# Laying down the engine orders of a four-stage attention kernel from new durations, and moving 32 PSUM copies to ScalarE

## The reference, cut to what matters

```python
x = x + tanh(g_xattn[0]) * L0_xattn(layernorm(x), ctx)   # 8 heads of 64, keys from ctx (512)
x = x + tanh(g_ffn[0])   * L0_ffn(layernorm(x))          # 16 heads of 8 over the 256 tokens, plus top-2 of 8 experts
x = x + tanh(g_xattn[1]) * L1_xattn(layernorm(x), ctx)   # 16 heads of 8, keys from ctx (512)
x = x + tanh(g_ffn[1])   * L1_ffn(layernorm(x))          # top-2 of 8 experts

def layernorm(x): return (x - mean(x)) / sqrt(var(x) + 1e-5)
def attend(q, k, v): return softmax(q @ k.T * scale) @ v          # per head
def experts(x): return sum over the two best gates of gate * (x @ W[e])
```

## Time and profile before

| | us |
|---|---|
| median of 3 runs | 804.36 |
| lowest and highest | 799.4, 807.34 |
| the profiled execution | 806.69 |
| its span, first to last instruction | 804.9 |
| TensorE busy in it | 683.4 (85%) |
| VectorE busy | 642.5 (80%) |
| ScalarE busy | 365.1 (45%) |
| GpSimd busy | 292.7 (36%) |
| TensorE's mean granted clock | 0.913 of full speed |

### The profile page before, as it was taken

One profiled execution on the slowest core, in us unless ns is written; L12 is line 12 of the kernel. 1 busy time (PEld: TensorE's weight loads), 2 busy tenths in 40 slices (PEclk: granted clock), 3 DMA queues, 4 the chain that ended last, 5 costly groups with the idle time before them and its releaser, 6 DMA issues.

```text
span 804.9 us, 13328 instructions
## 1 busy us (share of the span) xinstructions
PE 683.4 (85%) x5232; PEld 344.2 (43%) x5232; DVE 642.5 (80%) x1216; ACT 365.1 (45%) x450; POOL 292.7 (36%) x393
## 2 busy tenths in 40 slices
PE   4698999978989898988998898988979867877773
PEld 2354545533544354533544354534534423432331
DVE  1649788998878989798999999898887888858523
ACT  2352355224446645553547344553446445352340
POOL 6171843530633054323622363322622300613033
PEclk9799999977989999998999999997999969968596
DMA  6121102102010221112211211112120321021000
GB/s 169 59 80 42 54 19 81 40 8 74 17 30 30 60 71 60 39 30 86 61 50 38 68 41 59 32 31 86 35 67 32 96 65 57 18 91 37 2 7 7
DMA packets 45807, 40.84 MB, mean 51 GB/s; under 512 B 4840, under 2 KB 37552, under 8 KB 45744
## 3 DMA queue, kind: packets, MB, share of 16 engines
q1 hardware_dynamic: 45744, 39.98, 16.4%
HBM read 22.93 MB, written 17.04 MB: 50 GB/s over the span
## 4 chain that ended last, share of the span: by engine, by line
PE 53%; DVE 29%; ACT 7%; DMA 4%; issue 2%; SPq 2%; POOL 2%; POOLq 0%; DVEq 0%
PE psum L656 11%; DVE mx8B L901 5%; PE psum L568 5%; PE psum L612 4%; PE psum L576 4%; DVE mxA L824 4%; PE psum L644 4%; DVE mx8F L896 4%; ACT probB L713 4%; PE psum L543 4%; PE psum L538 3%; PE psum L625 3%; DVE rden L832 3%; DMA q8B<-q_dB 3%; PE psum L586 2%
## 5 line engine op out<-in xcount | busy, mean ns | idle before, releaser
L901 DVE TENSOR_REDUCE mx8B<-psum 128x2 f32<-128x1024 f32 x128 | 154.4, 1217 | 20.9 <-PE psum L625 20.1
L713 ACT ACTIVATE probB<-psum 128x1024 f32<-128x1024 f32 x128 | 126.1, 1024 | 89.9 <-PE psum L644 88.4
L700 ACT ACTIVATE probX<-psum 128x1024 f32<-128x1024 f32 x64 | 65.5, 1024 | 81.0 <-PE psum L568 80.2
L954 POOL TENSOR_TENSOR psum_k<-probX 128x512 f32<-128x512 f32 x32 | 41.0, 1281 | 120.1 <-ACT probX L700 119.2
L896 DVE TENSOR_REDUCE mx8F<-psum 128x4 f32<-128x1024 f32 x64 | 76.7, 1216 | 9.4 <-PE psum L619 9.2
L713 ACT ACTIVATE probF<-psum 128x1024 f32<-128x1024 f32 x64 | 65.1, 1026 | 37.5 <-PE psum L644 36.7
L824 DVE TENSOR_REDUCE mxA<-psum 128x2 f32<-128x1024 f32 x64 | 77.0, 1217 | 5.4 <-PE psum L550 5.0
L962 POOL TENSOR_TENSOR prodC<-prodC 128x256 f32<-128x256 f32 x32 | 24.4, 762 | 151.3 <-DVE prodC L889 151.2
L656 PE MATMUL psum<-probB,v8B 128*32 128x256 f32 x1024 | 72.7, 432 | 4.8 <-ACT probB L713 3.5
L832 DVE RECIPROCAL rden<-psum 128x256 f32<-128x256 f32 x32 | 56.1, 1752 | 19.4 <-PE psum L580 19.2
L568 PE MATMUL psum<-qX,kX 64*128 64x256 f32 x512 | 70.4, 397 | 0.0
(11 more groups left out here) (194 smaller groups left out, 1180.2 us busy)
## 6 DMA issues: line engine op xcount, KB each, us to landing
k8B<-k_dK SPq DMA_DIRECT2D x32, 192.0 KB
k_dK<-partsK SPq DMA_DIRECT2D x8, 384.0 KB, 2.6
q8F<-q_dF SPq DMA_DIRECT2D x32, 96.0 KB
k8F<-k_dF SPq DMA_DIRECT2D x32, 96.0 KB
q8B<-q_dB SPq DMA_DIRECT2D x32, 96.0 KB
k_dK<-partsK SPq DMA_DIRECT2D x8, 256.0 KB, 2.9
cTX<-in_ctxT SPq DMA_DIRECT2D x8, 192.0 KB, 2.4
cTK<-in_ctxT SPq DMA_DIRECT2D x8, 192.0 KB, 2.4
```

The source lines that it names most:

```text
L700: nc.scalar.activation(prob[s][(8 * b + k) % SLOTS[s]][:], ps, ACT.Exp, scale=float(XD) ** -0.5).then_inc(done["ACT"], 1)
L713: nc.scalar.activation(prob[s][(units * b + k) % SLOTS[s]][:], ps, ACT.Exp, scale=float(D8) ** -0.5).then_inc(done["ACT"], 1)
L901: nc.vector.tensor_reduce(mx8[s][:, t, :].rearrange("p (i q) -> p i q", i=2)[:, :, p], ps.rearrange("p (i n) -> p i n", i=2), AX.X, ALU.ma ...
```

## The change

The drain of every `ln` moves from VectorE to ScalarE: the branch with its waits goes from VectorE's program to ScalarE's, the copy becomes a `Copy` activation, and every dependence on it names ScalarE. The constants of the plan are replaced: `LAND` becomes one number per kind of transfer, and the durations of most fills are set to other values. Nothing else in the engines' programs is edited; since the orders and the banks come out of the plan, they can change everywhere.

```diff
-HOP, OUT, LAND = .07, .18, 2.0
+HOP, OUT = .07, .18
+LAND = {"xin": 2.1, "ctx": 2.5, "sw": 2.5, "mw": 1.5, "mr": 2.0, "out": 1.8, "sr": 3.5}
...
-    p.fill("DVE", 0, s, "ln", b, 0, .25, .43, [("DVE", s, "xh", b, 0)], last_use)
+    p.fill("ACT", 0, s, "ln", b, 0, .33, .42, [("DVE", s, "xh", b, 0)], last_use)
...
-    p.fill("ACT", 1, "X", "qp", b, 0, 1.85, 2.05, [("DVE", "X", "ln", b, 0)], ...
+    p.fill("ACT", 1, "X", "qp", b, 0, 1.85, 2.05, [("ACT", "X", "ln", b, 0)], ...
...
-        p.fill("DVE", 1, "X", "mx", b, k, .32, 1.23, ...
+        p.fill("DVE", 1, "X", "mx", b, k, .32, 1.22, ...
...
-        p.fill("ACT", 1, "X", "e", b, k, 1.25, 1.03, ...
+        p.fill("ACT", 1, "X", "e", b, k, 1.2, 1.03, ...
...
-        p.fill("DVE", 0, "X", "pv", b, k, 2.4, 2.2,
+        p.fill("DVE", 0, "X", "pv", b, k, 2.3, 2.2,
...
-    p.fill("DVE", 0, s, "gate", b, 0, .25, .85, [("DVE", s, "ln", b, 0)], ...
+    p.fill("DVE", 0, s, "gate", b, 0, .5, .85, [("ACT", s, "ln", b, 0)], ...
...
-        p.fill("DVE", 0, s, "moe", b, k, .9, .69, [("DVE", s, "ln", b, 0)], ...
+        p.fill("DVE", 0, s, "moe", b, k, 1.02, .69, [("ACT", s, "ln", b, 0)], ...
...
-        p.fill("DVE", 1, s, "mx8", b, k, .35, 1.25, ...
+        p.fill("DVE", 1, s, "mx8", b, k, .3, 1.22, ...
-    p.fill("DVE", 0, s, "mT8", b, 0, .25, .85, ...
+    p.fill("DVE", 0, s, "mT8", b, 0, .26, .85, ...
...
-        p.fill("ACT", 1, s, "e8", b, k, .4, 1.03, ...
+        p.fill("ACT", 1, s, "e8", b, k, .32, 1.03, ...
...
-        p.fill("ACT", 0, s, "pv8", b, k, .6 * n, .39, ...
+        p.fill("ACT", 0, s, "pv8", b, k, 1.0 if s == "F" else 1.87, .39, ...
...
-        p.fill("DVE", 0, s, "oT", b, k, .5, .95 if s == "F" else .58, ...
+        p.fill("DVE", 0, s, "oT", b, k, .55, .95 if s == "F" else .58, ...
...
-    p.fill("DVE", 0, "F", "v8", b, 0, .5, .43, [("DVE", "F", "ln", b, 0)], ...
+    p.fill("DVE", 0, "F", "v8", b, 0, .62, .43, [("ACT", "F", "ln", b, 0)], ...
...
 def slack(key):
-    return OUT if key[0] == "PE" else LAND if key[0] == "SP" else 0.
+    return OUT if key[0] == "PE" else LAND[key[2]] if key[0] == "SP" else 0.
...
@@ ScalarE's program @@
+                elif name == "ln":
+                    if s == "X":
+                        act.wait_ge(*is_full("X", "qp", b - 1))
+                    else:
+                        act.wait_ge(*is_full(s, "qk" if s == "B" else "moe", b - 1, 0 if s == "B" else 3))
+                        if s == "F":
+                            act.wait_ge(*is_full("F", "qk", b - 1))
+                            act.wait_ge(*is_full("F", "v8", b - 1))
+                    nc.scalar.activation(xT[s][:], ps[:, 0:SEQ], ACT.Copy).then_inc(done["ACT"], 1)
...
@@ VectorE's program @@
-                if name == "ln":
...
-                    nc.vector.tensor_copy(xT[s][:], ps[:, 0:SEQ]).then_inc(drained, 1)
-                elif name == "qk":
+                if name == "qk":
```

More of the change, by code:

```diff
@@ L68, in plan_x @@
     p.job("POOL", "X", "xb", b, 0, .75, ("SP", "X", "xin", b, 0), ("DVE", "X", "out", b - 1, 0))
-    p.fill("ACT", 1, "X", "qp", b, 0, 1.85, 2.05, [("DVE", "X", "ln", b, 0)], [("PE", "X", "e", b - 1, 7), ("PE", "X", "mx", b - 1, 7)])
+    p.fill("ACT", 1, "X", "qp", b, 0, 1.85, 2.05, [("ACT", "X", "ln", b, 0)], [("PE", "X", "e", b - 1, 7), ("PE", "X", "mx", b - 1, 7)])
     for k in range(2):
@@ L73, in plan_x @@
     for k in range(8):
-        p.fill("DVE", 1, "X", "mx", b, k, .32, 1.23, [("ACT", "X", "qp", b, 0), ("ACT", "X", "kp", b, k // 4)],
+        p.fill("DVE", 1, "X", "mx", b, k, .32, 1.22, [("ACT", "X", "qp", b, 0), ("ACT", "X", "kp", b, k // 4)],
                [("DVE", "X", "mT", b - 1, 0)])
@@ L80, in plan_x @@
         g = 8 * b + k - SLOTS["X"]
-        p.fill("ACT", 1, "X", "e", b, k, 1.25, 1.03, [("DVE", "X", "mT", b, 0), ("ACT", "X", "kp", b, k // 4)],
+        p.fill("ACT", 1, "X", "e", b, k, 1.2, 1.03, [("DVE", "X", "mT", b, 0), ("ACT", "X", "kp", b, k // 4)],
                [("PE", "X", "pv", g // 8, g % 8 // 2)])
@@ L92, in plan_gate @@
 def plan_gate(p, s, b, busy):
-    p.fill("DVE", 0, s, "gate", b, 0, .25, .85, [("DVE", s, "ln", b, 0)], [("DVE", s, "gx", b - 1, len(busy) - 1)])
+    p.fill("DVE", 0, s, "gate", b, 0, .5, .85, [("ACT", s, "ln", b, 0)], [("DVE", s, "gx", b - 1, len(busy) - 1)])
     p.job("ACT", s, "gx", b, 0, .25, ("DVE", s, "gate", b, 0))
@@ L101, in plan_moe @@
         freed = "POOL", s, "moe", b - (k < 2), (k - 2) % 4
-        p.fill("DVE", 0, s, "moe", b, k, .9, .69, [("DVE", s, "ln", b, 0)], [("DVE", s, "gx", b, last), freed])
+        p.fill("DVE", 0, s, "moe", b, k, 1.02, .69, [("ACT", s, "ln", b, 0)], [("DVE", s, "gx", b, last), freed])
         p.job("POOL", s, "moe", b, k, 1.65 if k % 2 else 1.2, ("DVE", s, "moe", b, k))
@@ L117, in plan_attend @@
     for k in range(maxima):
-        p.fill("DVE", 1, s, "mx8", b, k, .35, 1.25, [("SP", x, "sr", b, 2 * k // maxima) for x in stacked], [("DVE", s, "mT8", b - 1, 0)])
-    p.fill("DVE", 0, s, "mT8", b, 0, .25, .85, [("DVE", s, "mx8", b, maxima - 1)], [("SP", s, "mw", b - 1, 0)])
+        p.fill("DVE", 1, s, "mx8", b, k, .3, 1.22, [("SP", x, "sr", b, 2 * k // maxima) for x in stacked], [("DVE", s, "mT8", b - 1, 0)])
+    p.fill("DVE", 0, s, "mT8", b, 0, .26, .85, [("DVE", s, "mx8", b, maxima - 1)], [("SP", s, "mw", b - 1, 0)])
     p.job("SP", s, "mw", b, 0, .35, ("DVE", s, "mT8", b, 0), ("SP", s, "mr", b - 1, 0))
@@ L123, in plan_attend @@
         g = units * b + k - SLOTS[s]
-        p.fill("ACT", 1, s, "e8", b, k, .4, 1.03, [("SP", s, "mr", b, 0)], [("PE", s, "pv8", g // units, g % units // n)])
+        p.fill("ACT", 1, s, "e8", b, k, .32, 1.03, [("SP", s, "mr", b, 0)], [("PE", s, "pv8", g // units, g % units // n)])
     for k in range(4):
-        p.fill("ACT", 0, s, "pv8", b, k, .6 * n, .39, [("ACT", s, "e8", b, n * (k + 1) - 1), v], [("PE", s, "oT", b - 1, 1)])
+        p.fill("ACT", 0, s, "pv8", b, k, 1.0 if s == "F" else 1.87, .39, [("ACT", s, "e8", b, n * (k + 1) - 1), v], [("PE", s, "oT", b - 1, 1)])
     for k in range(QT):
-        p.fill("DVE", 0, s, "oT", b, k, .5, .95 if s == "F" else .58, [("ACT", s, "pv8", b, 3)], old)
+        p.fill("DVE", 0, s, "oT", b, k, .55, .95 if s == "F" else .58, [("ACT", s, "pv8", b, 3)], old)
 def plan_f(p, b):
     plan_norm(p, "F", b, ("DVE", "X", "out", b, 0), [("PE", "F", "moe", b - 1, 3)])
-    p.fill("ACT", 0, "F", "qk", b, 0, 1.0, 1.95, [("DVE", "F", "ln", b, 0)], [("SP", "F", "sw", b - 1, 0)])
+    p.fill("ACT", 0, "F", "qk", b, 0, 1.0, 1.95, [("ACT", "F", "ln", b, 0)], [("SP", "F", "sw", b - 1, 0)])
     plan_gate(p, "F", b, (1.2, .9, 1.1))
     plan_stack(p, "F", b, 1.85, 6, ("ACT", "F", "qk", b, 0), ("F", "e8"))
-    p.fill("DVE", 0, "F", "v8", b, 0, .5, .43, [("DVE", "F", "ln", b, 0)], [("PE", "F", "pv8", b - 1, 3)])
+    p.fill("DVE", 0, "F", "v8", b, 0, .62, .43, [("ACT", "F", "ln", b, 0)], [("PE", "F", "pv8", b - 1, 3)])
     plan_moe(p, "F", b, 2, ("DVE", "F", "oT", b - 1, 1))
-    p.fill("DVE", 0, "F", "wT", b, 0, .25, .4, [("DVE", "F", "gx", b, 2)])
-    p.fill("DVE", 0, "F", "wb", b, 0, .45, .49, [("DVE", "F", "wT", b, 0)], [("POOL", "F", "fin", b, 0)])
+    p.fill("DVE", 0, "F", "wT", b, 0, .3, .4, [("DVE", "F", "gx", b, 2)])
+    p.fill("DVE", 0, "F", "wb", b, 0, .64, .49, [("DVE", "F", "wT", b, 0)], [("POOL", "F", "fin", b, 0)])
     plan_attend(p, "F", b, "F", ("DVE", "F", "v8", b, 0), NPAIR,
@@ L148, in plan_k @@
     for k in range(2):
-        p.fill("DVE", 0, "K", "vv", b, k, .5, .43, [("SP", "K", "ctx", b, 0)], [("PE", "B", "pv8", b - 1, 3)])
+        p.fill("DVE", 0, "K", "vv", b, k, .58, .43, [("SP", "K", "ctx", b, 0)], [("PE", "B", "pv8", b - 1, 3)])
 def plan_b(p, b):
@@ L154, in plan_b @@
     p.job("POOL", "B", "xb", b, 0, .75, ("DVE", "F", "oT", b, 1), ("DVE", "B", "out8", b - 1, 0))
-    p.fill("DVE", 0, "B", "qk", b, 0, .5, 1.0, [("DVE", "B", "ln", b, 0)], [("SP", "B", "sw", b - 1, 0)])
+    p.fill("DVE", 0, "B", "qk", b, 0, .5, 1.0, [("ACT", "B", "ln", b, 0)], [("SP", "B", "sw", b - 1, 0)])
     plan_stack(p, "B", b, 1.35, 3, ("DVE", "B", "qk", b, 0), ("B", "e8"))
@@ L158, in plan_b @@
                 [("DVE", "B", "aT", b - 1, 0)])
-    p.fill("DVE", 0, "B", "aT", b, 0, .25, .43, [("DVE", "B", "oT", b, 1)], [("DVE", "B", "out8", b - 1, 0)])
-    p.fill("DVE", 0, "B", "out8", b, 0, .5, .49, [("DVE", "B", "aT", b, 0)], [("POOL", "B", "xb", b, 0), ("POOL", "C", "fin", b - 1, 0)])
+    p.fill("DVE", 0, "B", "aT", b, 0, .36, .43, [("DVE", "B", "oT", b, 1)], [("DVE", "B", "out8", b - 1, 0)])
+    p.fill("DVE", 0, "B", "out8", b, 0, .65, .49, [("DVE", "B", "aT", b, 0)], [("POOL", "B", "xb", b, 0), ("POOL", "C", "fin", b - 1, 0)])
 def plan_c(p, b):
```

## The result

The changed kernel takes 783.9 us (median of four runs, 781.3 to 784.9) against 805.7: a ratio of 0.9731, 95% interval 0.9687 to 0.9774, 2.7% faster. The forecast was 795 us, 1.2% faster, with 786 to 804 as its own range and 778 to 815 with all rivals. The sign was right. The size was not: the gain is over twice the forecast and lies outside the forecast's own range, inside the wide one.

What follows compares the result with a forecast made beforehand. TensorE's waits and VectorE's work were taken as the bound. Terms 3.9 + 2 + 3.5 + 0 = 9.4 us, off 806.7 us, gave 797.3, or 795 us against the median; own range 786 to 804, with rivals 778 to 815.

Steps and rivals of the forecast that it cites:

- all rivals: VectorE true limit, 779 us (0.16); TensorE limit, orders worth nothing, 804 us (0.20); lower TensorE clock, 817 us (0.16).
- Bound, and the end of the pipeline: TensorE and VectorE both about 90% full from 100 to 600 us; end from 700 us unpriced, 10 us change refutes.
- Part 1, the copies: 32 copies behind the transposes, 0.383 us each on ScalarE: 3.9 us from VectorE's relief, 2 us from TensorE's L590 waits.
- the 3.9 us from VectorE's share of the chain: 13.3 us of copies taken off VectorE, weighted by its 0.29 of the chain; ends 0 and 13.3.
- Part 2, landings: TensorE's idle time on q8B and k8F reloads falls from 7.0 to about 3.5 us, gaining 3.5 us; ends 0 and 7.0.
- The durations at 0 with ends of 12 us: New planned durations of TensorE's fills reorder all engines; gain taken as 0, with ends of 12 us either way.
- The sum of 9.4 us: Whole kernel: 3.9 for VectorE's copies, 2 for latency, 3.5 for landings, 0 for durations.
- the slower rival: New waits on TensorE lower its mean clock by 0.05, 22 us late, 817 us in all; chance 0.16.
- From 350 to 600 us: TensorE's share up from 90 to 91 or 92%, VectorE's down, clock at 0.95 or above.

Runs made afterwards that it cites:

- e3: Kernel before with its orders and banks kept word for word, only the copies moved to ScalarE: 806.9 us, ratio 1.000.
- e4: Changed kernel with its orders and banks kept word for word, the copies put back on VectorE: 802.1 us, 0.9997 of before.
- the families: First three draws within 0.5% of each table: old with copies on VectorE, mean ratio 1.0164 of before; new with copies on ScalarE, 1.0015.
- c_after: The changed kernel once more, unaltered, as control beside its draws on the same chip: 785.9 us, 0.9727 of before.
- c2_after: The changed kernel once more, unaltered, beside the best draw on the same chip: 790.8 us, 0.9787 of before.
- s10_after: Changed kernel replanned with each kind of job's duration varied within 0.5%, walk ending at 782.3 us: 795.6 us, 0.9856 of before.
- the best draw: Changed kernel replanned with durations varied within 3%, shortest walk of 1800 draws: 778.8 us, 0.9662 of before; again 779.7 us, 0.9653.

## Why the prediction was wrong

**Bound, and the end of the pipeline: right.** TensorE and VectorE still hold the chain, with 56% and 27%. The end, left unpriced, did stay as long as it was. The sign set for it, the stretch from 700 us on changing by 10 us, did show (104.9 to 82.0 us), but only because everything ahead of it ended earlier.

**Part 1, the copies: right in price, wrong in worth.** 0.38 us each, TensorE's idle time before L590's matmuls down by 3.4 us where I took 2. But the 3.9 us from VectorE's share of the chain have no counterpart: e3, the move in held orders, gives 1.000, and its walk is as long as that of before. An order that was made for a busier engine hands its freed time back as waits. In the new orders the same move decides 18 to 22 us (e4), more than the 13.3 us of work. What a moved instruction is worth is a property of the sequence around it; the chain's shares can't give it. VectorE's busy time fell by 20.8 us, 7.5 more than forecast, because its stretched instructions shrank on balance: K's subtraction lost 3.7 us and the xmid step 2.6, while `xhB` gained 2.2.

**Part 2, landings: right in kind.** The waits for q8B and k8F fell by 6.0 of 7.0 us, where I took half. The chain's pieces were miscounted: the wait for q8B at 597.07 us was taken twice, so there were five of them and one for k8F, 23.5 us and not 27.9. The term didn't rest on that sum. In the changed kernel one is left, of 4.0 us.

**The durations at 0 with ends of 12 us: the step that failed.** I reasoned that an error of half a us in the table is absorbed by the neighbour's queue. It is not: factors within 0.5% give other sequences, whose medians lie up to 30 us above the changed kernel's. That term needed ends of 25 us or more and not of 12. The list behind it was short as well: 192 `e8` fills and 192 `mx8` fills also came down, by 0.08 and 0.05 us each, and 32 `pv8` fills of F by 0.2, so that the plan's total for TensorE fell from 667.1 to 634.6 us. The sum of 9.4 us is close to the 12 us by which the two tables' draws differ, and to TensorE's 9.3 us less of idle time. It is near what the change is worth on average, and it was set against one draw of each, which lie apart by more. Part of that nearness is luck: the sum's 3.9 us for the copies weren't there in e3, and the orders, taken at 0, carry the families' 15 us of idle time.

**The clock: put at nothing in the sum, and seen with one sign only.** I made it the slower rival and priced a clock lower by 0.05 at 22 us. It went the other way: low clock fell from 140 to 111 us, which at 0.42 is 12 of the 13.6 us that TensorE's busy time lost. I had argued that the change removes waits, so the clock would at least not fall; by that argument a higher clock belonged in the forecast's own range. The families show the other side: with 15 us less idle time they have 13 us more of low clock, so the gain in clock is a property of this one sequence and not of the change. It repeats with it (121 and 122 us in c_after and c2_after). What lifts it is open. TensorE's total idle time doesn't tell it, as s10_after shows: only the best draw has less idle time, yet s10_after has 156 us of low clock. The Trainium skill (TensorE: Matmul & The Clock Gate, Why this matters for your kernels) names idle gaps between bursts of matmuls as what brings the lower clock. Which gaps those would be here no run shows.

**From 350 to 600 us** I expected TensorE at 91 to 92% (it is 92.4%) and the clock at 0.95 or above (0.99); VectorE less busy was wrong: it went from 226.6 to 229.5 us, since more batches' work fits in.

## What to carry to other kernels

When orders come out of a planner, one measured kernel is one draw: perturb its inputs within their own error, measure a few neighbours, and compare families before crediting an edit with a difference of 2 or 3%. The same spread can be used: stepping through the orders of many draws with measured durations and running the shortest gave 3.4% over before, the move of the copies included, and 0.7 to 1.3% over the changed kernel with nothing edited but the plan's durations. And split every difference into TensorE's busy and idle time; the first follows the granted clock and the second the order.

## What the runs showed of the hardware

The clock also goes with most of how one and the same kernel varies. Over 92 executions of the kernel before, run beside the experiments, spans run from 792.8 us at 106 us of low clock to 820.5 us at 181 us; the correlation is 0.93, with 0.32 us of span per us of low clock. Over 224 executions of all kernels, each taken against its own kernel's mean, it is 0.91 with the same slope. Three executions of 1195 to 1557 us are left out of this; they are not explained by it, since two of them have a granted clock of 1.0.
